# Causal attention on one core: the product with the values taken 512 queries at a time instead of 256, and the second group of the widest query tile copied a step later

## The reference, cut to what matters

```python
q = llama_rope(einsum('bsd,dnh->bsnh', x, wq)) / sqrt(128); k = llama_rope(einsum('bsd,dnh->bsnh', x, wk))
v = einsum('bsd,dnh->bsnh', x, wv)
logits = where(causal, einsum('bqnh,bknh->bnqk', q, k), -1e30)
probs = softmax(logits)
attn = einsum('bnqk,bknh->bqnh', probs, v)
x = x + einsum('bqnh,nhd->bqd', attn, wo)
```

## Time and profile before

| | us |
|---|---|
| Time, median of 3 runs (lowest to highest) | 1491.52 (1490.91 to 1491.75) |
| The profiled execution's own time | 1489.62 |
| Its span | 1487.5 |
| PE busy, share of the span | 95% |
| DVE, ACT, POOL busy, share of the span | 72%, 61%, 53% |
| Matmuls | 8932 |

### The profile page before, as it was taken

How to read it: one execution, slowest core, us unless ns; L and a number is a source line. 1 busy time by engine, 2 the same in 40 slices (tenths; PEclk the granted TensorE clock), 3 DMA queues, 4 the chain that set the end, 5 groups by cost and what they waited for, 6 DMA issues and landing times.

```text
span 1487.5 us, 25689 instructions
## 1 busy us (share of the span) xinstructions
PE 1419.2 (95%) x8932; PEld 1261.8 (85%) x8932; DVE 1072.3 (72%) x2395; ACT 912.1 (61%) x1890; POOL 782.8 (53%) x694
## 2 busy tenths in 40 slices
PE   6999999699999999999999999999999988999998
PEld 4778888589998999899989998999899877878886
DVE  7776876777767777777677767776777777775665
ACT  4544444577767767777777667776776654544433
POOL 4655454355555555555555555555555533755443
PEclk9999999899999999999999999999999999999999
DMA  4000001000000000000000000000000020000000
GB/s 167 1 1 1 1 1 50 22 7 23 1 8 15 8 8 8 15 9 8 15 2 8 22 1 8 22 1 8 8 1 1 1 111 1 1 15 1 15 15 15
DMA packets 11422, 23.40 MB, mean 16 GB/s; under 512 B 928, under 2 KB 5024, under 8 KB 11168
## 3 DMA queue, kind: packets, MB, share of 16 engines
q1 hardware_dynamic: 11296, 21.78, 4.4%
HBM read 19.68 MB, written 2.10 MB: 15 GB/s over the span
## 4 chain that ended last, share of the span: by engine, by line
PE 83%; DVE 9%; POOL 3%; issue 3%; ACT 1%; DMA 0%; DVEq 0%; POOLq 0%; ACTq 0%
PE ps L1439 24%; PE ps L1441 24%; PE ps L1440 24%; PE ps L1824 9%; DVE ps L1379 2%; DVE pT_l L327 1%; POOL um_l L327 1%; PE ps L1452 1%; POOL hid_l L327 1%; DVE hid L1079 1%; DVE mixed L1089 1%; POOL w_l L327 0%; POOL mixed_l L327 0%; DVE stats L934 0%; DVE xn L953 0%
## 5 line engine op out<-in xcount | busy, mean ns | idle before, releaser
L624 POOL TENSOR_SCALAR probs<-probs,inv_sum 128x128 f32<-128x128 f32 (+7 forms) x256 | 211.8, 828 | 387.1 <-DVE inv_sum L1314 387.1
L1379 DVE CUSTOM_DVE_ANT_0 ps<-ps,causal 128x128 f32<-128x128 f32 (+7 forms) x256 | 194.7, 761 | 211.0 <-PE ps L1441 209.2
L879 ACT ACTIVATE probs<-ps,neg_max 128x128 f32<-128x128 f32 (+7 forms) x256 | 189.1, 739 | 81.8 <-DVE neg_max L1379 81.8
L327 POOL TENSOR_TENSOR hid_l<-hid,hid_h 128x512 fp32r<-128x512 f32 x80 | 109.5, 1369 | 188.1 <-ACT hid_h L724 188.1
L327 DVE TENSOR_TENSOR pT_l<-ps,pT_h 128x512 fp32r<-128x512 f32 (+3 forms) x384 | 200.4, 549 | 2.8 <-ACT pT_h L858 2.6
L858 ACT ACTIVATE pT_h<-ps 128x512 fp32r<-128x512 f32 (+3 forms) x384 | 174.4, 491 | 34.6 <-PE ps L1824 32.1
L613 POOL TENSOR_TENSOR rot_sin<-swapped,rope 128x512 f32<-128x512 f32 x128 | 165.4, 1292 | 54.7 <-ACT swapped L835 54.7
L1824 PE MATMUL ps<-ident,probs 128*128 128x128 f32 x1152 | 170.9, 275 | 23.1 <-DVE pT_l L327 20.0
L1441 PE MATMUL ps<-pT_h,v_l 128*128 128x256 f32 (+1 forms) x640 | 179.0, 280 | 0.0
L1440 PE MATMUL ps<-pT_l,v_h 128*128 128x256 f32 (+1 forms) x640 | 178.9, 279 | 0.0
L1439 PE MATMUL ps<-pT_h,v_h 128*128 128x256 f32 (+1 forms) x640 | 178.1, 278 | 0.1
(11 more groups left out here) (190 smaller groups left out, 4076.4 us busy)
## 6 DMA issues: line engine op xcount, KB each, us to landing
w_raw<-attn_w SPq DMA_DIRECT2D x32, 256.0 KB, 2.6
w_in<-ffn_w SPq DMA_DIRECT2D x12, 576.0 KB, 8.3
x_sb<-x_in SPq DMA_DIRECT2D x4, 512.0 KB, 5.5
out<-x_sb SPq DMA_DIRECT2D x3, 512.0 KB, 3.2
rope<-rope_w SPq DMA_DIRECT2D x1, 1024.0 KB, 7.7
w_in<-ffn_w SPq DMA_DIRECT2D x2, 264.0 KB, 3.8
expand_raw<-expand_w SPq DMA_DIRECT2D x2, 256.0 KB, 4.8
out<-x_sb SPq DMA_DIRECT2D x2, 256.0 KB, 2.1
```

Source lines behind the costliest of these rows:

```text
L327: return eng.tensor_tensor(dst, src, high.bitcast(F32), ALU.subtract)
L624: pool.tensor_scalar(probs[s % 4][:, 0:n], probs[s % 4][:, 0:n], inv_sum[:, s % 4:s % 4 + 1], 1.0, ALU.mult, ALU.mult).then_inc(probs_read ...
L879: act.activation(probs[t % 4][:, 0:a * n].rearrange("p (a n) -> p a n", a=a), view, ACT.Exp, bias=neg_max[:, t % 4:t % 4 + 1], scale=-1.0, ...
L1379: dve.tensor_tensor_reduce(out=view, in0=view, in1=causal[:, SEQ - a * n:].rearrange("p (a n) -> p a n", a=a), scale=-SCALE, scalar=HUGE, ...
```

## The change

The probabilities are weighed in two chunks of 512 queries per unit, all in the unit that follows. Chunk 0 (key rows 0 to 3) goes in step 0; of chunk 1 key row 0 goes in step 3, rows 1 and 2 in step 4, rows 3 and 4 in step 5, rows 5 to 7 in step 6 (`PV_AT`). A row is one product of 512 columns, less on the diagonal (384, 256, 128). The attention output is copied in pieces of 512 columns, in step 1 (chunk 0) and step 7 (chunk 1) (`O_AT`). Output projections go to steps 3 and 5 of even units and 1 and 3 of odd units (`Y_AT`); the quarters of v go to steps 1 and 7 of even units and 5 and 7 of odd ones. Groups of transposes keep their number and sizes (12 per unit) but hold key tiles 0 to 3 first; of tile 7 the second group is copied by ScalarE and VectorE one step later than the first (`copies_of_step`). The transposed probabilities have new buffers (`before_h`, `before_l`, `own_h`, `own_l`), q has one buffer in place of two, with a wait on the scores that read it. The order in a step is as before but that the output projection comes ahead of `weigh`. The last pair's tables and its drain (8 steps in place of 9) are written anew.

```diff
-T_LAG, PV_LAG, OUT_LAG = 2, 5, 8
+T_LAG = 2
 ROPE_LAG = 2
-PAIR_SPLITS_AT = {"o": 7, "v": 17, "k": 21, "q": 23}
-DRAIN_STEPS = OUT_LAG + 1
-STATS_AT = [20, 21, 23, 24, 35, 37, 39]
-AGGREGATE_AT = [21, 24, 37]
-NORM_AT = [(23, 24), (25, 26), (38, 39)]
-TURN_AT, TURNED_LOW_AT = [(25, 25), (27, 29)], [(26, 27), (28, 31)]
+PAIR_SPLITS_AT = {"o": 13, "v": 25, "k": 21, "q": 23}
+DRAIN_STEPS = 8
+PV_AT = {0: (0, [0, 1, 2, 3]), 3: (1, [0]), 4: (1, [1, 2]), 5: (1, [3, 4]), 6: (1, [5, 6, 7])}
+O_AT = {1: 0, 7: 1}
+DRAIN_PV_AT = {32: (0, [0, 1, 2, 3]), 35: (1, [0, 1, 2, 3, 4, 5, 6, 7])}
+DRAIN_O_AT = {33: 0, 36: 1}
+Y_AT = {3: 0, 5: 1, 9: 2, 11: 3}
+LAST_Y_AT = [{19: 0, 21: 1, 24: 2, 25: 3}, {34: 0, 35: 1, 37: 2, 38: 3}]
...
-    first = 1 - i % 2
-    out = []
-    while first <= i + 1 - i % 2:
-        n = min(4, i + 2 - i % 2 - first)
-        out.append((first, n))
-        first += n
-    return out
+    return [(False, i + 1)] if i < 4 else [(True, 4), (False, i - 3)]
...
+        def turned_place(i, n, high):
+            is_before, count = tile_groups(i)[n]
+            if is_before:
+                at = P * (SEQ_TILES - 1 - i)
+                return (before_h if high else before_l)[:, :, at:at + P]
+            own, j = own_h if high else own_l, i % 4
+            if i < 4:
+                at, inner = P * j, 0
+            else:
+                at, inner = P * (17 - 4 * j), 2 * P
+            blocks = own[:, at:at + 3 * P * count].rearrange("p (a b) -> p a b", a=count)
+            return blocks[:, :, inner:inner + P]
+        def weighed_row(c, row):
+            if c == 1 and row < 4:
+                return slice(0, 512), (before_h[:, row], before_l[:, row])
+            d = row % 4
+            if c == 0:
+                cols, at = slice(P * d, 512), slice(4 * P * d, 4 * P * d + P * (4 - d))
+            else:
+                cols, at = slice(0, P * (4 - d)), slice(P * (16 - 3 * d), P * (20 - 4 * d))
+            return cols, (own_h[:, at], own_l[:, at])
...
-            if u % 2 == 1:
-                if u == UNITS - 1 and last:
-                    return None
+            if u % 2 == 0 and i in (1, 7):
+                k = 2 + i // 7
+                return "v", u // 2, 4 * (2 * p + u // 2) + k, k
+            if u % 2 == 1 and i in (5, 7) and not (u == UNITS - 1 and last):
+                k = i // 7
...
+        def unit_before(p, t, first):
+            if first and t < SEQ_TILES:
                 return None
-            q, s = tile
-            u, i = unit_of(s)
-            return u, i // 2, 16 * q + 4 * u + i // 2, q, s
-        def out_of_step(p, t, lag, first):
-            chunk = chunk_of_step(p, t, lag, first)
-            if not chunk or chunk[0] % 2 == 0:
+            return (p, t // SEQ_TILES - 1) if t >= SEQ_TILES else (p - 1, UNITS - 1)
...
+            c = O_AT.get(t % SEQ_TILES) if t < STEPS else DRAIN_O_AT.get(t)
+            return unit + (c, 8 * unit[0] + 2 * unit[1] + c) if unit and c is not None else None
...
+            if last:
+                for b in range(BATCH):
+                    if t in LAST_Y_AT[b]:
+                        return p, b, LAST_Y_AT[b][t], 4 * (2 * p + b) + LAST_Y_AT[b][t]
+            if t >= 2 * SEQ_TILES and t - 2 * SEQ_TILES in Y_AT and not last:
+                q, b, c = p, 0, Y_AT[t - 2 * SEQ_TILES]
+            elif t < 2 * SEQ_TILES and t in Y_AT and not first:
+                q, b, c = p - 1, 1, Y_AT[t]
+            else:
                 return None
-            u, c, _, q, _ = chunk
-            return u // 2, c, 4 * (2 * q + u // 2) + c, q
+            return q, b, c, 4 * (2 * q + b) + c
...
+        def copies_of_step(p, t, first):
+            late = tile_of_step(p, t, T_LAG + 2, first)
+            if late and late[1] % SEQ_TILES == SEQ_TILES - 1:
+                yield late + (1,)
+            tile = tile_of_step(p, t, T_LAG + 1, first)
+            if tile:
+                i = tile[1] % SEQ_TILES
+                for n in range(1 if i == SEQ_TILES - 1 else len(tile_groups(i))):
+                    yield tile + (n,)
...
+                if k % 2 == 1 and index >= 4:
+                    act.wait_ge(scores_done, SEQ_TILES * (index // 4 - 1) + 4 * (k // 2) + 4)
...
+                    for q, s, n in copies_of_step(p, t, first):
                         i = s % SEQ_TILES
-                        half = P * (i % 2)
-                        for n, (slot, count) in enumerate(tile_groups(i)):
-                            act.wait_ge(turned, groups_before(q, s) + n + 1)
-                            bank = T_BANK + (GROUPS_AT[i] + n) % 2
-                            act.activation(pT_h[i // 2 % 2][:, slot:slot + count, half:half + P],
-                                           ps[:, bank, 0:P * count].rearrange("p (a b) -> p a b", a=count),
-                                           ACT.Copy).then_inc(pT_high, 1)
+                        count = tile_groups(i)[n][1]
+                        act.wait_ge(turned, groups_before(q, s) + n + 1)
+                        bank = T_BANK + (GROUPS_AT[i] + n) % 2
+                        act.activation(turned_place(i, n, True),
+                                       ps[:, bank, 0:P * count].rearrange("p (a b) -> p a b", a=count),
+                                       ACT.Copy).then_inc(pT_high, 1)
...
+                        act.activation(o_place(u, c, True), ps[:, PV_BANK, :], ACT.Copy).then_inc(o_high, 1)
...
-                    y = out_of_step(p, t, OUT_LAG + 1, first)
+                    y = (y_of_step(p, t - 1, first, last) if t > 0 else None)
...
+                        low(dve, o_place(u, c, False), ps[:, PV_BANK, :], o_place(u, c, True)).then_inc(o_ready, 1)
...
-            def weigh(u, c, index, q, s, first_unit):
-                pe.wait_ge(pT_ready, groups_through(q, s))
-                need(pe, o_ready, index)
-                if first_unit:
-                    pe.wait_ge(v_ready, c + 1)
-                elif c == 0 and u % 2 == 0:
+            def weigh(q, u, c, rows, first_unit):
+                final = 3 + 4 * c
+                index = 8 * q + 2 * u + c
+                if rows[0] == 0:
+                    need(pe, o_ready, index)
+                if c == 0:
+                    pe.wait_ge(pT_ready, groups_through(q, SEQ_TILES * u + 3))
+                elif rows[0] == 0:
+                    pe.wait_ge(pT_ready, groups_through(q, SEQ_TILES * u + 7) - 1)
+                if c == 1 and 4 in rows:
+                    pe.wait_ge(pT_ready, groups_through(q, SEQ_TILES * u + 7))
+                if u % 2 == 0 and c == 0:
+                    pe.wait_ge(v_ready, 2 if first_unit else 4 * (2 * q + u // 2) + 2)
+                elif u % 2 == 0 and 4 in rows:
                     pe.wait_ge(v_ready, 4 * (2 * q + u // 2) + 4)
                 head, b = u % 2, u // 2
-                order = [1, 0] + list(range(2, 2 * c + 2))
-                for slot in order:
-                    kt = 2 * c + 1 - slot
-                    w = tuple(v[:, b, kt, HD * head:HD * head + HD] for v in (v_h, v_l))
-                    q = slice(P if slot == 0 else 0, 2 * P)
-                    ins = product(ps[:, PV_BANK, q], w, (pT_h[c % 2][:, slot, q], pT_l[c % 2][:, slot, q]),
-                                  slot == order[0], slot == order[-1], skip=True)
-                ins.then_inc(pv_done, 1)
-            def project_out(b, c, index, q, bank):
+                for row in rows:
+                    w = tuple(v[:, b, row, HD * head:HD * head + HD] for v in (v_h, v_l))
+                    cols, probabilities = weighed_row(c, row)
+                    ins = product(ps[:, PV_BANK, cols], w, probabilities, row == 0, row == final, skip=True)
+                if rows[-1] == final:
+                    ins.then_inc(pv_done, 1)
+            def project_out(q, b, c, index, bank):
...
-                    chunk = chunk_of_step(p, t, PV_LAG, first)
-                    if chunk:
-                        weigh(*chunk, first and chunk[0] == 0)
-                    y = out_of_step(p, t, OUT_LAG, first)
+                    y = y_of_step(p, t, first, last)
                     if y:
-                        project_out(*y, misc_bank(t))
+                        project_out(*y, y_bank(p, t, last))
+                    work = weigh_of_step(p, t, first)
+                    if work:
+                        weigh(*work, first and t < 2 * SEQ_TILES)
...
```

More of the change, by code:

```diff
@@ new lines, in weigh_of_step, with o_of_step, o_place @@
+        def weigh_of_step(p, t, first):
+            unit = unit_before(p, t, first)
+            work = PV_AT.get(t % SEQ_TILES) if t < STEPS else DRAIN_PV_AT.get(t)
+            return unit + work if unit and work else None
+        def o_of_step(p, t, first):
+            unit = unit_before(p, t, first)
+            c = O_AT.get(t % SEQ_TILES) if t < STEPS else DRAIN_O_AT.get(t)
+            return unit + (c, 8 * unit[0] + 2 * unit[1] + c) if unit and c is not None else None
+        def o_place(u, c, high):
```

(8 more changed lines are left out.)

104 lines of the change are left out of this document (51 added, 53 removed).

## The result

The changed kernel takes 1512.12 us (median of 4 runs, 1511.86 to 1514.31) against 1491.24 (1490.91 to 1491.75) for the kernel before on the same chip: a ratio of 1.0143, 95% interval 1.0125 to 1.0160. It is 20.9 us slower. The forecast was 1503, 11.5 slower, range 1488 to 1514. The direction was right and the time lies in the stated range, but near its slow end and outside the 1497 to 1510 that the forecast itself was given: what came is nearly twice what was forecast. The profiled execution has a span of 1509.7, 22.2 more than before.

What follows compares the result with a forecast made beforehand. TensorE's own work was taken to set the pace in attention. Value products -14.7, step 2 stalls +23.5 and ends +2.7 gave +11.5 on 1489.62, so 1501.1; the median lies 1.9 higher, 1503.0. Range 1488 to 1514, the forecast's own 1497 to 1510.

Steps and rivals of the forecast that it cites:

- Part 1: Products with the values, cut into fewer, wider matmuls: 6.96 to 6.50 us a unit, a gain of 14.7 us.
- The rival price of 2 us in all: Value products estimated by the skill's formula: a gain of 2 us in all instead of 14.7, time about 1516.
- Part 3, step 2: Tile 0's transposes stall for VectorE's low part: 1.08 us with v in step 1, 0.52 with a projection; 23.5 in all.
- Rival A: VectorE reaches step 2's first low part before TensorE needs it, so it comes out faster, about 1480 us; chance 0.18.
- B: Part of step 2's stall goes, as the v copy or rotation sum comes earlier: 1491 to 1492 us; chance 0.08.
- Step 7: One side item and the same VectorE chain as before: TensorE's idle 0.88 us in each step 7 stays.
- Part 3, step 3: Tile 1's transposes, which need the delayed second group's bank: TensorE arrives after they are possible, covered by 0.36 us.
- has slack: ScalarE over a unit: its sum of work falls as well, and it has slack.
- rival C: Step 3's cover of 0.36 fails too, or 512-wide products save little: 12 us per 0.4 a unit, 1515; chance 0.10.
- The delay itself costs nothing: Copying tile 7's second group one step later has no cost, as it is read first in step 3.
- was in nobody's way: The 0.60 us that the delay takes out of VectorE's step 2 stood behind the critical low part, hindering nobody.
- Part 4, the ends: First pair's second unit and the last pair, with work moved and waits changed: +2.7 us, range -1 to +7.

Runs made afterwards that it cites:

- the kernel of the three edits: Changed kernel with low parts ahead of the minimum in step 7, step 1's output low part in two halves, step 35's projection in bank 4: 1486.04 us, ratio 0.9961.

## Why the prediction was right, and where its sizes were off

- **Part 1 was right.** The products with the values take 6.51 us a unit (forecast 6.50, before 6.96), and wide ones stand 0.23 apart (638.90 to 639.13). The rival price of 2 us in all, an estimate from the formula that the Trainium skill (TensorE: Matmul & The Clock Gate, Back-to-back issue gap) gives for an isolated matmul, is refuted by these rows for this stream, although the time it gave, 1516, is nearer to the result than 1503: it would have come out near for the wrong reason. In 32 units the gain is 14.4 us, and the waits ate it.
- **Part 3, step 2: right in place and size.** Waits of 1.05 and 0.51 against 1.08 and 0.52, in all 23 us. Halving the copy took 0.27 from both, so the chain was the right one. Rival A is out, and so is B.
- **Step 7: right.** 0.83 from the low part at 635.66 (VectorE) to the transposes at 636.49, a wait of 0.87, unchanged. In the kernel before, part of it stood elsewhere: in units with v in step 7 the first matmul of v started 0.50 behind the last one of the scores, of which 0.23 is that one's own, and only 0.50 was left in front of the transposes. So not all of the rise from 20.0 to 47 us in the list of waits is new waiting:

```profile
687.88 0.40 PE L1441 MATMUL ps<-qk,qk 128*128 128x512 f32 x1
688.38 0.39 PE L1439 MATMUL ps<-wv_h,xnT_h 128*128 128x256 f32 x1
```

- **Part 3, step 3: wrong.** "Covered by 0.36" is a wait of 0.20, 6 us in 30 units. I counted VectorE's minimum and its length, and took ScalarE's high part as made. VectorE and ScalarE in step 3 of the changed kernel:

```profile
647.05 0.68 DVE L1368 TENSOR_TENSOR rot<-ps,rope 128x512 f32<-128x512 f32 x1
...
649.62 0.89 DVE L337 TENSOR_TENSOR own_l<-ps,own_h 128x512 fp32r<-128x512 f32 x2 [0.42 <-ACT own_h L932]
```

```profile
647.77 0.59 ACT L908 ACTIVATE swapped<-ps 64x512 f32<-64x512 f32 x1 [0.47 <-DVE rot L1368]
648.37 0.59 ACT L909 ACTIVATE swapped<-ps 64x512 f32<-64x512 f32 x1
648.99 0.77 ACT L932 ACTIVATE own_h<-ps 128x512 fp32r<-128x512 f32 x2
```

  The high part stood behind two swaps on ScalarE, and these waited for VectorE's cosine product, which stands behind step 2's critical low part. So the low part of step 3 started 0.57 behind the end of the minimum (649.05 to 649.62; the profile lists 0.42 of it as idle), for a copy on another engine that was itself late because of step 2; 0.57 less the cover of 0.36 is the 0.20. That ScalarE "has slack" was said of its sum, and the sum is not what counts. This is rival C at half its size, by ScalarE's queue and not by VectorE's own.
- **"The delay itself costs nothing", and the 0.60 "was in nobody's way": wrong in both halves.** In the new order it costs 0.20 in step 3, and put back it costs 0.3 in step 5, 4 us more in all. Alone, in the kernel before, the delay costs 10.6.
- **Part 4, the ends: mis-sized.** Forecast +2.7 (-1 to +7), the profiles show about +5, and 1.7 more that is a matter of the execution and not of the change. From the profiles: up to step 7 of the last pair's third unit the changed kernel is 15.4 us later, of which -13.5 + 23 + 6 explain all; its last unit gives back 1.6, and from tile 7's last transposes to those of the next layer norm it takes 31.0 instead of 24.3. These are the rows of the two kernels, before and after:

```profile
1232.21 1.03 PE L1824 MATMUL ps<-ident,probs 128*128 128x128 f32 x8
...
1256.53 1.91 PE L1452 MATMUL ps<-ident,xn 128*128 128x128 f32 x8
```

```profile
1246.05 1.04 PE L1893 MATMUL ps<-ident,probs 128*128 128x128 f32 x8
...
1277.06 1.91 PE L1520 MATMUL ps<-ident,xn 128*128 128x128 f32 x8
```

  I had counted waits of steps 24 to 27 (step 26's came as forecast, 1.63 against 1.6, step 27's longer, 1.74 against 1.1) and none of the drain, whose order is written anew. Its two waits in series, with a lower clock behind them, cost most of the 6.7: with both taken away the stretch is 26.5 long (1221.30 to 1247.81), and the time falls 5.4 in two steps (1.5 and 3.9, on different bases).

  The last 1.7 us of the span's 22.2 stand right behind the drain and are clock. In the changed kernel's profile matmuls of 512 columns start 0.43 apart there (1283.68 to 1284.11); the kernel with low parts first in step 7, whose program is the same from there on, has the full clock. Windows of the changed kernel and of that one:

```profile
1283.00:1289.00 6.00, 5.75 (x23) 4.31 (x23) 3.77 (x9) 2.56 (x6) 0.00 (x0) 0.74 0.00 1
```

```profile
1265.00:1271.00 6.00, 5.75 (x30) 4.51 (x28) 5.31 (x9) 3.71 (x6) 1.65 (x2) 1.00 0.01 4
```

  From that layer norm's transposes to the end of the program the latter takes 231.1 us, the kernel before 231.0, the changed one 232.7.
- **The sum.** -14.4 + 23 + 6 + 5 = +20, with the 1.7 of clock +22, on spans of 1487.5 and 1509.7; the medians are 20.9 apart. The forecast lacked 6 in step 3 and 2.4 in the ends. That the time still fell into the range is owed to the range's width: the sum had no term for a wait in step 3. What stays open: the 2.2 us by which the drain is still longer with both waits gone (26.5 against 24.3) were not traced to an instruction.

## What to carry to other kernels

A wait on a copy is fed by every engine that the copy passes through: count the queue of each (here ScalarE's swaps and high parts ahead of VectorE's low parts), not only of the one that the profile names as releaser. An edit of order has no price of its own; the same delay or the same swap of two instructions changed its sign with what TensorE had to do in the step where the lateness came out, so after a change of cover the old order is to be tried again. Where the end of a program is written anew, walk through it bank by bank as through the steady part.

## What the runs showed of the hardware that was not expected

A wait in the drain cost more than its length, since the clock fell behind it; but whether it fell, and where, was not the same in each kernel with the same wait. In the changed kernel TensorE idles 3.06 us, and the window behind has a granted clock of 0.72, a mixture of the two levels, 1.2 and 2.4 GHz; at its start matmuls of 256 columns stand 0.21 apart (1252.72, 1252.94) instead of 0.12, which is 256 columns at 1.2 GHz. With the projection in bank 4 and an idle stretch of 2.06 instead, the same window has 1.00. The windows of 1252 to 1258, first of the changed kernel, then of that one (busy PE, PEld, DVE, ACT, POOL, granted clock, DMA share, GB/s):

```profile
1252.00:1258.00 6.00, 5.63 (x24) 5.13 (x25) 0.82 (x2) 0.00 (x0) 0.00 (x0) 0.72 0.01 3
```

```profile
1252.00:1258.00 6.00, 3.94 (x19) 3.17 (x19) 2.15 (x11) 0.00 (x0) 0.18 (x1) 1.00 0.01 3
```

The twelve matmuls of that projection lost about 12 x 0.09 = 1.1 us to it. But the 2.06 us did not spare the clock by being shorter: in the kernel of the three edits, with the same 2.06 in front of the same products (1229.84), the clock fell too, and its matmuls of 512 columns stand 0.43 apart (1230.61, 1231.03) in place of 0.23:

```profile
1230.00:1236.00 6.00, 6.00 (x23) 4.91 (x23) 0.00 (x0) 0.00 (x0) 0.00 (x0) 0.72 0.01 3
```

Over all profiles: the six kernels that idle 3 us or more in front of that projection all have a window of 0.72 to 0.74 behind it, at a cost of 1.1 to 1.6 us, in some of them only after part of the projection has run at full clock; of the three that idle 2.06 two have it (1.3 and 1.6 us) and one has not; the two without a wait there have 1.00. These rows make no rule for how long an idle stretch may be. They show that a wait can cost a third to three quarters of its length more in clock, and that the same code can be some 1.6 us apart by it between two profiles (behind the drain, above).
